# A GRU scan on one core: the new state summed by a reduction over adjacent pairs instead of an addition of two tiles

## The reference, cut to what matters

```python
def cell(h, x):
    gi = x @ W_ih + b_ih
    gh = h @ W_hh + b_hh
    i_r, i_z, i_n = jnp.split(gi, 3, axis=-1)
    h_r, h_z, h_n = jnp.split(gh, 3, axis=-1)
    r = jax.nn.sigmoid(i_r + h_r)
    z = jax.nn.sigmoid(i_z + h_z)
    n = jnp.tanh(i_n + r * h_n)
    h_new = (1.0 - z) * n + z * h
    return (h_new, h_new)
_, hs = jax.lax.scan(cell, initial_state, xs)      # 512 steps, one after the other
```

## Time and profile before

| | |
|---|---|
| median of 3 runs | 3007.75 us (3006.93 to 3011.0) |
| the profiled execution | 3008.64 us |
| its span, first to last instruction | 3006.8 us |
| scan, block 0 (from about 764 us) | 64 steps, 234 us |
| scan, blocks 1 to 7 (998 to 2857 us) | 448 steps, with the feed-forward layer beside it |
| last feed-forward block alone | from about 2857 us, 150 us |

### The profile page before, as it was taken

How to read it: one execution, slowest core, us unless ns; L and a number is a source line. 1 busy time by engine, 2 the same in 40 slices (tenths; PEclk the granted TensorE clock), 3 DMA queues, 4 the chain that set the end, 5 groups by cost and what they waited for, 6 DMA issues and landing times.

```text
span 3006.8 us, 158572 instructions
## 1 busy us (share of the span) xinstructions
PE 2679.4 (89%) x69122; PEld 1975.4 (66%) x69122; DVE 2183.7 (73%) x7136; ACT 1056.4 (35%) x3485; POOL 1231.2 (41%) x2955
## 2 busy tenths in 40 slices
PE   5599898987899899899989998998999899899999
PEld 2344343433555677777777777777777777777788
DVE  4667666571566788888888888888888888888832
ACT  3452636261122233333333333333333333333333
POOL 0441312021222355455545544544555455455544
PEclk9599999998899999999999999999999999999999
DMA  4102010102210224323332432243243224322244
GB/s 168 60 2 47 3 33 13 26 20 56 41 14 4 62 81 89 89 80 85 88 88 80 93 83 84 83 91 86 83 92 88 80 81 91 88 82 83 81 140 134
DMA packets 271431, 215.83 MB, mean 72 GB/s; under 512 B 162576, under 2 KB 214032, under 8 KB 270352
## 3 DMA queue, kind: packets, MB, share of 16 engines
q1 hardware_dynamic: 269584, 201.49, 25.5%
q10 hardware_dynamic: 1152, 4.19, 0.3%
HBM read 188.85 MB, written 16.78 MB: 68 GB/s over the span
## 4 chain that ended last, share of the span: by engine, by line
PE 38%; DVE 27%; issue 5%; ACT 3%; POOL 1%; DMA 1%; DVEq 0%; SPq 0%; POOLq 0%; ACTq 0%
PE ps L1034 25%; PE ps L1056 7%; DVE h L945 6%; DVE turn_n L930 4%; DVE turn L933 4%; PE ps L1069 4%; DVE npre L936 4%; ACT cand L841 3%; DVE fresh L942 3%; DVE hcur L944 3%; DVE hcur L947 2%; PE ps L1045 1%; DMA gi<-gi_scratch 0%; POOL hid L779 0%; DMA w<-in_w 0%
## 5 line engine op out<-in xcount | busy, mean ns | idle before, releaser
L1034 PE MATMUL ps<-whh,hcur 128*32 128x128 f16 x49152 | 790.7, 221 | 168.7 <-DVE hcur L947 143.5
L1034 PEld LDWEIGHTS ps<-whh,hcur 128*32 128x32 f16 x49152 | 699.2, 97 | 319.1 <-DVE hcur L947 285.4
L1056 PE MATMUL ps<-hb,w 128*128 128x256 f16 x6400 | 812.6, 274 | 2.5 <-issue 2.0
L1056 PEld LDWEIGHTS ps<-hb,w 128*128 128x128 bf16 x6400 | 605.8, 98 | 103.4 <-issue 6.2
L834 ACT ACTIVATE r<-ur 128x16 f32<-128x16 f32 x512 | 110.6, 216 | 1007.3 <-DVE ur L924 1007.3
L1069 PE MATMUL ps<-hid,w 128*128 128x256 f16 x3200 | 435.4, 273 | 14.9 <-POOL hid L779 14.9
L779 POOL TENSOR_TENSOR hid<-hidf,hid 128x256 f16<-128x256 f32 x400 | 268.6, 671 | 346.6 <-ACT hid L830 346.6
L767 POOL TENSOR_TENSOR hidf<-up 128x256 f32<-128x256 f32 x400 | 292.9, 732 | 169.1 <-DVE up L915 151.6
L1069 PEld LDWEIGHTS ps<-hid,w 128*128 128x128 bf16 x3200 | 298.5, 98 | 69.4 <-issue 18.7
L759 POOL COPY hb<-hcur 128x32 f16<-128x32 f16 x512 | 170.5, 333 | 320.6 <-DVE hcur L947 320.6
L921 DVE STREAM_TRANSPOSE turn<-ps 128x128 f32<-128x128 f32 x512 | 162.3, 317 | 172.9 <-PE ps L1034 161.3
(11 more groups left out here) (139 smaller groups left out, 3333.7 us busy)
## 6 DMA issues: line engine op xcount, KB each, us to landing
w<-in_w SPq DMA_DIRECT2D x400, 256.0 KB, 2.7
w<-in_w SPq DMA_DIRECT2D x400, 128.0 KB, 2.4
gi_scratch<-stage SPq DMA_DIRECT2D x48, 256.0 KB, 2.6
gi<-gi_scratch SPq DMA_DIRECT2D x16, 768.0 KB, 9.4
x2T<-in_xT SPq DMA_DIRECT2D x4, 1024.0 KB, 7.6
out<-xo ACTq DMA_DIRECT2D x8, 512.0 KB, 3.1
stage<-in_W_hh SPq DMA_DIRECT2D x1, 3072.0 KB, 10.9
x2T<-in_W_ih SPq DMA_DIRECT2D x1, 3072.0 KB, 11.8
```

What stands on the lines that cost most here:

```text
L1034: mm = pe.matmul(ps[j * COLS:(j + 1) * COLS, bank, 0:P], hcur[:, k], whh[:, s, k, at:at + P], start=(k + s == 0), stop=(k == KT - 1 and s ...
L1056: mm = pe.matmul(ps[:, UB[u], w * TOK:(w + 1) * TOK], w13[:, u, w, k], hb[:, f % 2, s, k].rearrange("p b t -> p (b t)"), start=(w + k + s ...
```

## The change

`zh` and `fresh` were two contiguous tiles of 128 x 16 float32. They become the even and the odd elements of one tile `terms` of 128 x 16 x 2. The two products write into it with a step of two elements (L939, L942), `hi` reads it with that step (L944), and `h` is made by a `tensor_reduce` that adds each adjacent pair (L945), in place of a `tensor_tensor` addition of the two tiles. No instruction is added, taken away or moved, and all waits are the same.

```diff
-        zh = sb("zh", [P, KT, B], F32)
+        terms = sb("terms", [P, KT, B, 2], F32)
...
-        fresh = sb("fresh", [P, KT, B], F32)
...
+        zh, fresh = terms[:, :, :, 0], terms[:, :, :, 1]
...
                 dve.wait_ge(z_ready, 2 * g + 2)
-                nc.vector.tensor_tensor(zh[:], z[:], h[:], ALU.mult).then_inc(kept, 1)
+                nc.vector.tensor_tensor(zh, z[:], h[:], ALU.mult).then_inc(kept, 1)
                 dve.wait_ge(kept, g + 1)
                 dve.wait_ge(cand_ready, g + 1)
-                nc.vector.tensor_tensor(fresh[:], cand[:], omz[:], ALU.mult).then_inc(fresh_done, 1)
+                nc.vector.tensor_tensor(fresh, cand[:], omz[:], ALU.mult).then_inc(fresh_done, 1)
                 dve.wait_ge(fresh_done, g * 3 + 1)
-                nc.vector.tensor_tensor(hi, fresh[:], zh[:], ALU.add).then_inc(fresh_done, 1)
-                nc.vector.tensor_tensor(h[:], fresh[:], zh[:], ALU.add).then_inc(fresh_done, 1)
+                nc.vector.tensor_tensor(hi, fresh, zh, ALU.add).then_inc(fresh_done, 1)
+                nc.vector.tensor_reduce(h[:], terms[:], AX.X, ALU.add).then_inc(fresh_done, 1)
                 dve.wait_ge(fresh_done, g * 3 + 3)
                 nc.vector.tensor_tensor(lo, h[:], hi, ALU.subtract).then_inc(h_ready, 1)
```

## The result

The changed kernel takes 2955.56 us in the median of 4 runs (2951.7 to 2959.16), the kernel before 3009.38 in 4 runs (3006.93 to 3012.36). The ratio is 0.9821, 95% interval 0.98 to 0.9841: 53.8 us less, outside what a measurement can confuse with no change. The forecast was 2953, range 2938 to 2969. The profiled execution took 2959.16 us, with a span of 2957.1, so 49.5 us less than the profiled one of before; it is one of the two slower of the four runs. Between the first and the last `lo` of the scan it is 48.7 us shorter than before; the other 1 us of the span lies in stages that the change doesn't touch.

A forecast was written before the change was run, and what follows sets the result against it. It took the chain through TensorE's scan matmuls and VectorE's L945, held by GpSimd's L779, as the bound. 3008.64 - 58.9 (held steps) + 4 (other steps) = 2953.7 us, median 2953; range 2938 to 2969.

The forecast's parts named there:

- The hold: VectorE's L945: a two-SBUF-tile tensor_tensor started while GpSimd's L779 runs doesn't finish before it; 668 ns against 169.
- lo is the next to be held: L947, behind h: held by L779 instead, ending at 1505.25, 0.03 behind it, not 1505.45; gain 0.20 us.
- The gain in held steps: TensorE's scan starts behind a held h: 251 x 0.20 + 62 x 0.14 + 17 x 0 = 58.9 us less.
- the sign: TensorE's idle time before L1034 in the scan: shorter by about 59 us.
- The cost in the other steps: L945 where not held: reduction 210 ns against 169, 101 steps x 0.04 = 4 us more.
- The step of two: Strided access in zh, fresh and hi: taken as 0, range 0 to 0.03 us for each of fresh and hi.
- B: Slower rival at L944: hi loses its 0.06 us lead, falls behind L779 and is held; 3065 us, chance 0.07.
- A: Rival at L947: lo isn't held by L779 and ends 0.46 us earlier; 2901 us, chance 0.05.
- C: Rival at L945: the reduction is held by L779 too; 3008 to 3025 us, chance 0.07.

The follow-up runs named there:

- the swap: The changed kernel with hi (L944) and the reduction (L945) in swapped order: 3010.43 us, ratio 1.0 to the kernel before.

## Why the prediction was right

- **The hold.** "It is not something about L945": shown by runs that change the kind of instruction, the order, the place and the length of L779 and the place of an input; in each the lines were held or free as the theory said. One count was off: L779 came before `hi` in 10 steps, with 0.53 to 0.70 us, not in 8; nothing in the sum hangs on it.
- **lo is the next to be held.** No row of before showed L947 held. It is, and ends 0.03 behind L779, the figure predicted. In one number the prediction contradicted itself: it gave 0.57 us for L947's median, but by its own two times (1504.82 to 1505.25) it is 0.43. Measured: 0.454. The sum used the times, so nothing else hung on the slip.
- **The gain in held steps.** Forecast 58.9 us. Taking the steps of the two timelines pairwise from the end of one `lo` to that of the next, the 327 steps that are held in both are 58.3 us shorter together. Of these, 224 gain 0.19 to 0.25 us, 47.2 together (forecast 251 x 0.20 = 50.2), and 62 gain 0.10 to 0.19, 8.6 together, since TensorE's list becomes the bound there (forecast 62 x 0.14 = 8.7); 23 gain nothing (forecast 17), and 18 differ by other amounts, 2.6 together. TensorE's idle time put down to L947 falls from 143.5 to 83.3 us, 60.2 less, against the 59 that was named as the sign.
- **The cost in the other steps.** Mis-sized: the reduction was taken as 0.21 us and is 0.177 to 0.179, against the addition's 0.169. Over 101 steps that is 1 us, not 4; block 0 is 0.1 us longer in all, not 2 to 3. The reason is the choice of row: the price of 261 for 64 values was scaled down, but the row for 32 values in and 2 out (186) was the nearer one.
- **The step of two.** Taken as 0: right. `fresh` is 177 against 176, `hi` 176 against 175 in the median. Hence `hi` kept its lead and B didn't happen; but the swap shows that the lead of 0.06 us carries the whole result.
- **What it missed.** Three steps in which `lo` had just escaped are held now, as the reduction puts `lo` 0.01 us later. One of them, before and after:

```profile
1977.84 0.17 DVE L947 TENSOR_TENSOR hcur<-h,hcur 128x16 f16<-128x16 f32 x1
1977.84 0.71 POOL L779 TENSOR_TENSOR hid<-hidf,hid 128x256 f16<-128x256 f32 x1 [1.04 <-ACT hid L830]
```

```profile
1952.35 0.67 POOL L779 TENSOR_TENSOR hid<-hidf,hid 128x256 f16<-128x256 f32 x1 [1.05 <-ACT hid L830]
1952.35 0.69 DVE L947 TENSOR_TENSOR hcur<-h,hcur 128x16 f16<-128x16 f32 x1
```

  Both start in the same hundredth: `lo` 3 ns ahead of L779 before, 7 ns behind it after. Once VectorE wins and GpSimd's instruction is 0.04 us longer than its usual 0.67; once GpSimd wins and VectorE's takes 0.69. The three steps are 1.6 us longer together, part of which the steps behind them give back. The other thing missed is the pair of steps behind the load of `gi`, 6.6 us in the profiled pair and 2 us by medians.
- **What is luck.** The held steps were right in mechanism, in kind and in size. That the total came out within 3 us owes something to errors that cancel: a cost of 4 us where 1 was paid stood in for the newly held steps and the load, which the sum didn't have.
- **A hold that nobody counted.** The product with r (L933) has 48 values a partition and reads two SBUF tiles, and in 477 of 512 steps it starts 0.02 to 0.04 us behind GpSimd's L775, which takes 0.22. Such a call takes 288 ns in the median, the 35 others 241. Both kinds, in the kernel before:

```profile
1503.32 0.22 POOL L775 TENSOR_TENSOR uz<-zs,turn 128x16 f32<-128x16 f32 x1
1503.34 0.29 DVE L933 TENSOR_TENSOR turn<-turn_n,r 128x48 f32<-128x48 f32 x1
```

```profile
1696.03 0.22 POOL L775 TENSOR_TENSOR uz<-zs,turn 128x16 f32<-128x16 f32 x1
1696.13 0.24 DVE L933 TENSOR_TENSOR turn<-turn_n,r 128x48 f32<-128x48 f32 x1
```

  In those 477 calls it ends 0.09 to 0.12 us behind L775, not 0.03. The excess over 240 ns is 24 us in all, and the same in the changed kernel (470 calls), on a line that has 4% and 3% of the two chains. So it has no part in the difference. No run moved L775 alone; that the two lines are tied is read from these times, and what untying them would give is not shown.
- **The rivals.** A fell (`lo` is held with both inputs in SBUF). Its price was too large: with the hold gone by any of three ways, the kernels come to 2909 to 2920, against the 2901 worked out. Some of that is the load of `gi`: the two steps behind it take 70.9 us in the kernel with 2909, 7.4 more than before. The rest is not taken apart. C fell: 187 ns is the reduction's maximum beside L779.

## What to carry to other kernels

When one instruction on a chain takes several times what its twin beside it takes, look in the timeline for what another engine runs at that moment, and where it ends: if the two ends keep the same small distance in call after call (here 0.03 us in all 340 held calls of before), the instruction isn't dear, it is held. Then ask which instruction behind it is the next to be held: the gain is what had stood behind the held one, here 0.20 us, and not the length of the hold, 0.50. The cure that goes further is to leave the instructions that meet the other engine with one SBUF input each (zh and h in PSUM, 2909 us), or to move the other engine's work off that moment (2918 to 2920), at the price of whoever waits for that work.

## What the runs showed of the hardware

- A `tensor_tensor` on VectorE with two SBUF inputs of 16 values that starts 0.01 to 0.38 us behind GpSimd's L779 (two SBUF inputs of 256 values, 0.67 us) ends 0.03 us behind it, with inputs and outputs of float32 or float16. One of 48 values behind GpSimd's L775 (16 values, 0.22 us) ends 0.09 to 0.12 behind. With one input in PSUM, or as a reduction of one tile, an instruction of this size keeps to 0.17 to 0.20 us.
- Who holds whom is a matter of nanoseconds of a start. In all traces with L779 in its old place, a VectorE instruction of this kind that started 0 to 4 ns behind L779 ran through (174 to 177 ns); from 6 ns on it was held; at 5 ns both happened. Where it ran through and the starts lay within 5 ns, an L779 of 256 columns took 707 to 720 ns in place of 671.
- Operands of 16 values in PSUM cost little on VectorE here: 170 to 179 ns, against 168 to 176 with all in SBUF. A reduction with its output in PSUM takes 187 against 179, but with its output in SBUF and ahead of `hi` it took 186 as well.
- Reading or writing 16 float32 values with a step of two costs 1 ns at most (177 against 176 for `fresh`, 176 against 175 for `hi`).
